# Last expert's bias products in its first layer and each normalisation one tile later; first expert's sums from its own rows

## The chip, the cores and the metric

The kernel runs on one NeuronCore of a Trainium2 chip. The metric is the device time of one execution in microseconds, the median of several. Its engines work side by side and meet at semaphores: TensorE (PE, with its weight loads as PEld), VectorE (DVE), ScalarE (ACT), GpSimd (POOL) and SyncE (SP). POOL issues the indirect DMAs (rows picked by an index), SP the plain loads. "POOLq" and "SPq" are the sequencers of these engines.

## The reference

One transformer layer on 4 x 1024 tokens of width 256: attention with 16 heads, an add and a layer norm, then a mixture of 8 experts, top 2, capacity 1280 rows each, an add and a layer norm. The change touches the second half only:

```python
x = _layernorm(x + attention(x))                       # (4, 1024, 256)
gates = softmax(x_flat @ router_w + router_b)          # (4096, 8)
expert_mask = one_hot(top2(gates)).sum(1)
pos = cumsum(expert_mask, axis=0) - 1                  # a token's slot in its expert
valid = expert_mask * (pos < capacity) > 0
buf[e, pos] = x_flat[token]                            # 8 x 1280 rows
h = gelu(buf[e] @ w1[e] + b1[e])
out = h @ w2[e] + b2[e]
y[token] = sum over its experts e of gates[token, e] * out[e, pos]
x = _layernorm(x + y)
```

## The kernel before, in words

`attention` (lines 144 to 1448) computes the first half. It leaves, in HBM, every token's row in `dispatched` (a row of 265 numbers for each slot of each expert: the token's 256 values, its 8 gates, its number) and in `sum_scratch`, where one row per token starts as the token's own values and collects the experts' outputs. Slots that no token fills hold zeros and an index of their own, behind the tokens.

`experts` (lines 1465 to 1903) handles the eight experts one after another, each 1280 rows as ST = 5 tiles of 128. LAST is expert 7. fp32 products are made of three (high by high, high by low, low by high), so every operand is split into a high part (ScalarE) and a remainder (VectorE). Per expert e:

- SP (`load_rows`, `load_weights`) loads the expert's rows into `rows[e % 2]` and its two weight matrices into `raw1`, `raw2`, in program order on one queue: rows of e, first weights of e, second weights of e, rows of e + 1. From expert 2 on, rows wait for `s_index >= e - 1` (line 1523).
- TensorE runs the first layer, 8 blocks m of 12 matmuls into `hp` (line 1663), then the second, 5 tiles t, each 8 high products (line 1629) and 8 low ones (line 1639) into `yp`. Between the tiles it transposes the next expert's rows (line 1617). Tile t waits until VectorE has read `yp` of tile t - 2 (`s_z`, line 1625).
- ScalarE applies Gelu to each block (line 1742) and copies the high part (line 1748), then takes the logarithm and exponential for the inverse deviations of the expert before (`rstd_guess`, lines 1717 and 1719), splits the next expert's weights and rows, and normalises the outputs of the expert before (`normalise`, line 1727).
- VectorE makes each block's remainder (line 1878), the index of the rows after block 1 (`index`), and, behind blocks 2 to 6, the statistics of the expert before (`variance`, lines 1824 and 1825; `tell_variances`, line 1829). In the second layer, for each tile: `prepare` (line 1845) puts gate times output bias onto the sums gathered from `sum_scratch`, into `others`; `add_own` (lines 1854 and 1856) adds gate times `yp`, into `eo`. `scale_and_shift` does one Newton step on the inverse deviation (lines 1459 to 1462) and the shift (line 1836).
- POOL, in its own fixed order: gathers the five tiles of sums (`gather_sums`, line 1557), tile t behind block t + 3 of the first layer; stores the new sums (`store_sums`, line 1565) and the normalised rows of the expert before (`store_outputs`, line 1574). A store of sums by one expert is waited for before the next expert gathers.

So the normalised rows of every expert are stored to `out`; the last expert that holds a token writes its final row. The last expert has no successor to hide behind: there VectorE works tile by tile (lines 1889 to 1902): `prepare` t, then (from tile 1) the Newton step of tile t - 1, for which it waits on ScalarE, `add_own` t, statistics of t. ScalarE answers each tile with `rstd_guess` and `normalise` (lines 1765 to 1767), and POOL stores it. `link` makes VectorE wait for the end of one of its own instructions before the next.

```python
                    if e == LAST and t:
                        scale_and_shift(LAST + t - 1, e, slice(t - 1, t))
```

The functions that the change touches:

Of the kernel before, what the change touches and what calls it, by code (L numbers as in the profile page):

```python
# [9 lines left out]
ALU = mybir.AluOpType  # L10
# [4 lines left out]
BATCH, SEQ, DIM, HEADS = 4, 1024, 256, 16  # L15
# [1449 lines left out]
def experts(nc, w1_d, b1_d, w2_d, b2_d, tile_d, disp_d, sum_d, ident, areas, out):  # L1465

    with ExitStack() as ctx:
# [40 lines left out]
        s_gather = [sem(f"s_gather{t}") for t in range(ST)]  # L1508
        s_sum, s_out = sem("s_sum"), sem("s_out")
        s_var, s_rstd, s_shift, s_final = sem("s_var2"), sem("s_rstd2"), sem("s_shift"), sem("s_final")  # L1510
        s_chain, s_actchain = sem("s_chain2"), sem("s_actchain2")
        block = ctx.enter_context(nc.Block())

# [4 lines left out]
        @block.sync  # L1518
        def _(sp):
            def load_rows(e):  # L1520
                if e >= 2:

                    sp.wait_ge(s_index, e - 1)
                sp.dma_start(rows[e % 2], disp_d[e * CAP:(e + 1) * CAP].rearrange("(t p) d -> p t d", p=P)
                             ).then_inc(s_rows[e % 2], 16)

            def load_weights(e):
                if e >= 2:

                    sp.wait_ge(s_w1lo, KC * (e - 1))  # L1530
                else:
                    sp.wait_ge(s_first_lo, KC)
                sp.dma_start(raw1, w1_d[e].rearrange("(k p) n -> p k n", p=P)).then_inc(s_w1, 16)
                if e >= 2:

                    sp.wait_ge(s_w2lo, KC * (e - 1))
                else:
                    sp.wait_ge(s_first_lo, 2 * KC)
                sp.dma_start(raw2, w2_d[e].rearrange("(k p) n -> p k n", p=P)).then_inc(s_w2, 16)

            for t in range(ST):
                sp.dma_start(rows[0][:, t], disp_d[P * t:P * (t + 1)]).then_inc(s_first[t], 16)
            sp.dma_start(b1[:], b1_d).then_inc(s_b1, 16)
            sp.dma_start(tile_no[:], tile_d).then_inc(s_tile, 16)
            load_rows(1)
            load_weights(1)
            sp.dma_start(b2[:].rearrange("p e d -> p (e d)"), b2_d.to_broadcast((P, EXPERTS * DIM))
                         ).then_inc(s_bias, 16)
            for e in range(2, EXPERTS):
                load_rows(e)  # L1550
                load_weights(e)

        @block.gpsimd
        def _(pool):
            def gather_sums(e, t):

                pool.indirect_dma_start(  # L1557
                    others[:, t, :], None, sum_d,
                    bass.IndirectOffsetOnAxis(ap=add_idx[e % 3][:, t:t + 1], axis=0),
                    bounds_check=TOKENS + CAP - 1).then_inc(s_gather[t], 16)  # L1560

            def store_sums(e, t):

                pool.wait_ge(s_z, ST * e + t + 1)
                pool.indirect_dma_start(  # L1565
                    sum_d, bass.IndirectOffsetOnAxis(ap=add_idx[e % 3][:, t:t + 1], axis=0),
                    eo[e % 2][:, t, :], None, bounds_check=TOKENS + CAP - 1).then_inc(s_sum, 16)

            def store_outputs(e, t):

                pool.wait_ge(s_final, ST * e + t + 1)
                if t == 0 and e:
                    pool.wait_ge(s_out, 16 * ST * e)
                pool.indirect_dma_start(  # L1574
                    rows_out, bass.IndirectOffsetOnAxis(ap=add_idx[e % 3][:, t:t + 1], axis=0),
                    eo[e % 2][:, t, :], None, bounds_check=TOKENS - 1, oob_is_err=False).then_inc(s_out, 16)

            for e in range(EXPERTS):
                if e:
                    store_sums(e - 1, ST - 1)  # L1580
                if e >= 2:
                    pool.wait_ge(s_h, HK * e + 2)
                    store_outputs(e - 2, 3)
                pool.wait_ge(s_index, e + 1)
                if e:
                    pool.wait_ge(s_sum, 16 * ST * e)
                    pool.wait_ge(s_z, ST * e)
                for t in range(ST):
                    pool.wait_ge(s_h, HK * e + 3 + t)
                    gather_sums(e, t)  # L1590
                if e >= 2:
                    pool.wait_ge(s_h, HK * (e + 1))
                    store_outputs(e - 2, 4)
                for t in range(ST - 1):
                    if e < LAST:
                        store_sums(e, t)
                    if e and t:
                        store_outputs(e - 1, t - 1)
            for t in range(ST - 2, ST):
                store_outputs(LAST - 1, t)  # L1600
            for t in range(ST):
                store_outputs(LAST, t)
            pool.wait_ge(s_out, 16 * ST * EXPERTS)
# [85 lines left out]
        def _(act):  # L1689
# [74 lines left out]
                    act.preload_act_table(ACT.Gelu)  # L1764
            for t in range(ST):
                rstd_guess(LAST + t, LAST, slice(t, t + 1))
                normalise(LAST + t, LAST, (t,))

        @block.vector
        def _(dve):  # L1770
            links = [0]

            def link(ins):
                links[0] += 1
                ins.then_inc(s_chain, 1)
                dve.wait_ge(s_chain, links[0])
# [50 lines left out]
            def tell_variances(n, e, T):  # L1827

                dve.tensor_scalar(lnt[e % 2][:, 0, T], mv[e % 2][:, T, 1], EPS, None, ALU.add).then_inc(s_var, 1)
                dve.wait_ge(s_var, n + 1)  # L1830

            def scale_and_shift(n, e, T):

                dve.wait_ge(s_rstd, n + 1)
                newton(dve, link, lnt[e % 2][:, :, T])
                dve.scalar_tensor_tensor(lnt[e % 2][:, 5, T], mv[e % 2][:, T, 0], -1.0, lnt[e % 2][:, 4, T],
                                         ALU.mult, ALU.mult).then_inc(s_shift, 1)

            def prepare(e, t):

                n, g = ST * e + t, gate[e % 2][:, t:t + 1]
                if n == 0:
                    dve.wait_ge(s_bias, 16)
                dve.wait_ge(s_gather[t], 16 * (e + 1))
                link(dve.scalar_tensor_tensor(others[:, t, :], b2[:, e, :], g, others[:, t, :], ALU.mult, ALU.add))  # L1845

            def add_own(e, t):

# [22 lines left out]
            for e in range(EXPERTS):  # L1871
                for m in range(HK):
# [8 lines left out]
                        index(e)  # L1881
                    if e and 2 <= m < 2 + ST:
                        variance(e - 1, m - 2)
                if e:
                    tell_variances(e - 1, e - 1, slice(0, ST))
                for t in range(ST):
                    if e + 1 < EXPERTS and t >= 2:
                        turned(e + 1, t)
                    prepare(e, t)
                    if e and t == 0:  # L1890
                        scale_and_shift(e - 1, e - 1, slice(0, ST))
                    if e == LAST and t:
                        scale_and_shift(LAST + t - 1, e, slice(t - 1, t))
                    add_own(e, t)
                    if e + 1 < EXPERTS:
                        if t < 2:
# [3 lines left out]
                    if e == LAST:  # L1900
                        variance(e, t)
                        tell_variances(LAST + t, e, slice(t, t + 1))
            scale_and_shift(LAST + ST - 1, LAST, slice(ST - 1, ST))


# [54 lines left out]
```

## Time and profile before

| | |
|---|---|
| time, median of 3 runs | 938.64 us (938.22 to 940.34) |
| time of the profiled execution | 938.71 us |
| its span, first to last instruction | 936.93 us |
| the experts' part of the span | 681.3 to 936.9 us |
| PE busy / DVE busy / ACT busy / POOL busy | 95% / 68% / 78% / 53% |
| granted TensorE clock, mean | 0.981 |

The span starts at the first instruction, and times below count from there in microseconds. The time of an execution is the span and some 1.8 us around it. A timeline row shows start, duration, engine, line, operation, the tile written and the tiles read, and in square brackets how long the engine had been idle and what ended that. Lines of the changed kernel are higher by 1 to 22: L1829 there is L1834, L1845 is L1867, L1854 is L1876, L1856 is L1878, L1717 is L1721, L1727 is L1731, L1574 is L1578.

### The profile page before, as it was taken

To read this page: it belongs to the slowest core of one execution; us is meant where nothing else is said; L and a number is where in the kernel's file an instruction comes from. 1 tells how busy PE (TensorE), PEld (TensorE's weight loads), DVE (VectorE), ACT (ScalarE), POOL (GpSimd) and SP (SyncE) were. 2 spreads that over 40 slices of the span, in tenths; PEclk is the share of its full clock that TensorE was granted. 3 is DMA by queue.
4 is the path that set the end of the run, shared out by engine and by line. 5 is a ranking of instruction groups with operands and counts; after the bars stand their busy time and mean duration, and the time that the engine had idled before them with its cause. 6 is when DMAs were issued, how large, how long until landed. Compare 5 with 4: busy or idle time off the path is not lost. (4 is left out here: it accounts for less than half of the span.)

```text
span 936.9 us, 19456 instructions
## 1 busy us (share of the span) xinstructions
PE 893.0 (95%) x7345; PEld 508.7 (54%) x7345; DVE 635.9 (68%) x1193; ACT 731.7 (78%) x894; POOL 496.1 (53%) x412
## 2 busy tenths in 40 slices
PE   8899998999999999999999999999589999999994
PEld 5434343434334434333443433344489999998993
DVE  5678555557886655889565676437457877888876
ACT  6688977897797899789789879987265787777863
POOL 5478344245475745747564444522623656656564
PEclk9899999999999999999999999999799999999998
DMA  5724495442446335253433426531274435534311
GB/s 175 171 89 159 144 302 192 146 166 96 154 141 226 114 132 215 84 197 124 163 129 133 146 97 207 167 105 36 90 242 138 134 131 176 175 137 140 121 60 56
DMA packets 62713, 136.08 MB, mean 145 GB/s; under 512 B 10370, under 2 KB 31427, under 8 KB 62480
## 3 DMA queue, kind: packets, MB, share of 16 engines
q1 hardware_dynamic: 41936, 72.88, 23.9%
q0 software_dynamic: 20672, 61.83, 19.1%
q8 instruction: 61, 1.00, 0.4%
q14 instruction: 44, 0.36, 0.1%
HBM read 69.85 MB, written 62.35 MB: 141 GB/s over the span
## 5 line engine op out<-in xcount | busy, mean ns | idle before, releaser
L788 ACT ACTIVATE prob<-spsum 128x1024 f32<-128x1024 f32 x512 | 493.6, 1022 | 92.0 <-PE spsum L992 86.2
L1016 PE MATMUL opsum<-prob,val 128*17 128x512 f32 x2048 | 271.3, 599 | 3.0 <-DVE oraw L1391 2.2
L992 PEld LDWEIGHTS spsum<-stacks 32*128 32x128 f32 x1536 | 73.7, 184 | 116.3 <-ACT prob L788 63.6
L992 PE MATMUL spsum<-stacks 32*128 32x512 f32 x1536 | 133.3, 427 | 3.0 <-DMA stacks<-split_scratch 2.4
L992 PEld LDWEIGHTS spsum<-area_q 32*128 32x128 f32 x1536 | 73.6, 185 | 112.3 <-ACT prob L788 65.3
L992 PE MATMUL spsum<-area_q 32*128 32x512 f32 x1536 | 133.3, 429 | 0.8 <-ACT prob L788 0.7
L1399 DVE RECIPROCAL oden<-oden 128x256 f32<-128x256 f32 x62 | 108.7, 1753 | 2.1
L667 POOL TENSOR_TENSOR onorm<-oraw,oden 128x512 f32<-128x512 f32 x31 | 42.0, 1356 | 104.9 <-DVE oden L1399 104.8
L581 POOL TENSOR_TENSOR area_s<-emb,area_s 128x1024 fp32r<-128x1024 f32 x28 | 66.6, 2380 | 50.2 <-DVE area_s L1210 50.2
L625 POOL DMA_INDIRECT dispatched<-res,scatter_idx x64 | 64.9, 1014 | 48.1 <-issue 24.7
L579 POOL TENSOR_TENSOR square<-raw 128x512 bf16<-128x512 f32 x28 | 53.9, 1924 | 58.5 <-DVE raw L1190 58.4
L1016 PEld LDWEIGHTS opsum<-prob,val 128*17 128x17 f32 x2048 | 36.1, 95 | 89.2 <-ACT prob L788 51.5
L1557 POOL DMA_INDIRECT others<-sum_scratch,add_idx x40 | 57.0, 1424 | 42.2 <-PE hp L1663 41.3
L1742 ACT ACTIVATE hraw<-hp,b 128x640 f32<-128x640 f32 x64 | 51.0, 797 | 31.8 <-PE hp L1663 30.6
L1878 DVE TENSOR_TENSOR hid<-hraw,hid 128x640 fp32r<-128x640 f32 x64 | 52.8, 825 | 29.9 <-ACT hid L1748 29.9
L1565 POOL DMA_INDIRECT sum_scratch<-eo,add_idx x35 | 44.1, 1261 | 44.5 <-DVE eo L1856 36.9
L1391 DVE COPY oraw<-opsum 128x512 f32<-128x512 f32 x31 | 21.4, 692 | 58.1 <-PE opsum L1016 57.7
L1663 PE MATMUL hp<-xe,area_s 128*128 128x320 f32 x384 | 57.1, 309 | 0.5 <-DVE xe L1788 0.5
L1663 PE MATMUL hp<-xe,w1s 128*128 128x320 f32 x384 | 57.0, 308 | 0.0
L1663 PEld LDWEIGHTS hp<-xe,area_s 128*128 128x128 f32 x384 | 56.4, 188 | 0.7 <-issue 0.7
L1663 PEld LDWEIGHTS hp<-xe,w1s 128*128 128x128 f32 x384 | 56.4, 188 | 0.0
L1574 POOL DMA_INDIRECT out<-eo,add_idx x40 | 41.7, 1042 | 25.6 <-issue 13.7
(246 smaller groups left out, 1371.0 us busy)
## 6 DMA issues: line engine op xcount, KB each, us to landing
split_scratch<-area_s POOLq DMA_DIRECT2D x56, 512.0 KB, 4.1
area_k<-in_w SPq DMA_DIRECT2D x16, 1024.0 KB, 5.3
area_q<-split_scratch SPq DMA_DIRECT2D x28, 512.0 KB, 5.6
stacks<-split_scratch SPq DMA_DIRECT2D x24, 512.0 KB, 5.3
dispatched<-res POOLq DMA_DIRECT2D x1, 5300.0 KB, 27.8
rows<-dispatched SPq DMA_DIRECT2D x7, 662.5 KB, 5.4
res<-in_x SPq DMA_DIRECT2D x4, 1024.0 KB, 8.6
aT<-onorm SPq DMA_DIRECT2D x124, 32.0 KB
```

The costliest lines, as they stand in the source:

```text
L579: pool.tensor_tensor(square[:, i], raw[:], raw[:], ALU.mult).then_inc(s_square, 1)
L581: pool.tensor_tensor(split[u % 2][:, 1], embs[u % 2][:], split[u % 2][:, 0].bitcast(F32), ALU.subtract).then_inc(s_split, 1)
L625: pool.indirect_dma_start(disp_d, bass.IndirectOffsetOnAxis(ap=scatter_idx[:, k, t:t + 1], axis=0), ress[UNITS[u][0] % 2][:, t, :], None, ...
L788: act.activation(prob[u % NPB][:], spsum[u % NSB][:].rearrange("p a n -> p (a n)"), ACT.Exp, scale=HD ** -0.5).then_inc(s_exp, 1)
L992: ins = pe.matmul(spsum[u % NSB][:, j % 2, :], kst[par][rows, a, P * kt:P * (kt + 1)], qst[par][rows, b, cols], start=i == 0, stop=i == 2 ...
L1016: ins = pe.matmul(opsum[32 * j:32 * j + HD + 1, :], val[b % 2][:, kt, h0 + j, :], prob[(2 * s + j // 2) % NPB][:, HALF * (j % 2):HALF * (j ...
L1399: tell(dve.reciprocal(half, half), s_sums)
L1557: pool.indirect_dma_start(others[:, t, :], None, sum_d, bass.IndirectOffsetOnAxis(ap=add_idx[e % 3][:, t:t + 1], axis=0), bounds_check=TOK ...
L1565: pool.indirect_dma_start(sum_d, bass.IndirectOffsetOnAxis(ap=add_idx[e % 3][:, t:t + 1], axis=0), eo[e % 2][:, t, :], None, bounds_check= ...
L1663: ins = pe.matmul(hp[n % 2][:, h, 0:CH], w1s[e % 2][:, b, k, P * m:P * (m + 1)], xe[e % 2][:, a, k, CH * h:CH * (h + 1)], start=k == 0 and ...
L1742: act.activation(hraw[n % NH][:].rearrange("p (h n) -> p h n", h=2), hp[n % 2][:, :, 0:CH], ACT.Gelu, bias=b1[:, e, m:m + 1]).then_inc(s_g ...
L1878: dve.tensor_tensor(hids[:, 1, m], hraw[n % NH][:], hids[:, 0, m].bitcast(F32), ALU.subtract).then_inc(s_hid, 1)
```

## The change

Three things, all in `experts`:

1. *Last expert, bias products.* `prepare` of tiles 0, 1 and 2 moves into the first layer, behind blocks 5, 6 and 7; that of tiles 3 and 4 runs behind the statistics of tiles 0 and 1.
2. *Last expert, scales.* The Newton step and shift of tile t - 1 (`finish_tile`, new, with the first two of its instructions merged into one) run behind the statistics of tile t, not ahead of `add_own` of t. On ScalarE the normalisation of tile t - 1 follows `rstd_guess` of tile t. Tile 4 is normalised by VectorE itself, in one `tensor_scalar` on the tile, and its store waits for the new semaphore `s_tail`.
3. *First expert.* No gathers: `prepare` reads the expert's own rows in `rows[0]` (no expert has added anything yet). Those rows are now read until the end of expert 0, so expert 2's rows, which go to the same place, wait for `s_index >= 2` instead of 1; and `s_gather` counts one expert less.

```diff
--- before.py
+++ after.py
@@ -1508,6 +1508,7 @@
         s_gather = [sem(f"s_gather{t}") for t in range(ST)]
         s_sum, s_out = sem("s_sum"), sem("s_out")
         s_var, s_rstd, s_shift, s_final = sem("s_var2"), sem("s_rstd2"), sem("s_shift"), sem("s_final")
+        s_tail = sem("s_tail")
         s_chain, s_actchain = sem("s_chain2"), sem("s_actchain2")
         block = ctx.enter_context(nc.Block())
 
@@ -1520,7 +1521,7 @@
             def load_rows(e):
                 if e >= 2:
 
-                    sp.wait_ge(s_index, e - 1)
+                    sp.wait_ge(s_index, max(e - 1, 2))
                 sp.dma_start(rows[e % 2], disp_d[e * CAP:(e + 1) * CAP].rearrange("(t p) d -> p t d", p=P)
                              ).then_inc(s_rows[e % 2], 16)
 
@@ -1568,7 +1569,10 @@
 
             def store_outputs(e, t):
 
-                pool.wait_ge(s_final, ST * e + t + 1)
+                if e == LAST and t == ST - 1:
+                    pool.wait_ge(s_tail, 1)
+                else:
+                    pool.wait_ge(s_final, ST * e + t + 1)
                 if t == 0 and e:
                     pool.wait_ge(s_out, 16 * ST * e)
                 pool.indirect_dma_start(
@@ -1585,7 +1589,7 @@
                 if e:
                     pool.wait_ge(s_sum, 16 * ST * e)
                     pool.wait_ge(s_z, ST * e)
-                for t in range(ST):
+                for t in range(ST if e else 0):
                     pool.wait_ge(s_h, HK * e + 3 + t)
                     gather_sums(e, t)
                 if e >= 2:
@@ -1764,7 +1768,8 @@
                     act.preload_act_table(ACT.Gelu)
             for t in range(ST):
                 rstd_guess(LAST + t, LAST, slice(t, t + 1))
-                normalise(LAST + t, LAST, (t,))
+                if t:
+                    normalise(LAST + t - 1, LAST, (t - 1,))
 
         @block.vector
         def _(dve):
@@ -1829,6 +1834,21 @@
                 dve.tensor_scalar(lnt[e % 2][:, 0, T], mv[e % 2][:, T, 1], EPS, None, ALU.add).then_inc(s_var, 1)
                 dve.wait_ge(s_var, n + 1)
 
+            def finish_tile(e, t):
+
+                n, T = LAST + t, slice(t, t + 1)
+                v, guess, w, rstd, shift = (lnt[e % 2][:, i, T] for i in (0, 2, 3, 4, 5))
+                dve.wait_ge(s_rstd, n + 1)
+                link(dve.scalar_tensor_tensor(w, guess, guess, v, ALU.mult, ALU.mult))
+                link(dve.tensor_scalar(w, w, -0.5, 1.5, ALU.mult, ALU.add))
+                link(dve.tensor_tensor(rstd, guess, w, ALU.mult))
+                if t < ST - 1:
+                    dve.scalar_tensor_tensor(shift, mv[e % 2][:, t, 0:1], -1.0, rstd, ALU.mult, ALU.mult
+                                             ).then_inc(s_shift, 1)
+                else:
+                    dve.tensor_scalar(eo[e % 2][:, t, :], eo[e % 2][:, t, :], mv[e % 2][:, t, 0:1], rstd,
+                                      ALU.subtract, ALU.mult).then_inc(s_tail, 1)
+
             def scale_and_shift(n, e, T):
 
                 dve.wait_ge(s_rstd, n + 1)
@@ -1841,8 +1861,10 @@
                 n, g = ST * e + t, gate[e % 2][:, t:t + 1]
                 if n == 0:
                     dve.wait_ge(s_bias, 16)
-                dve.wait_ge(s_gather[t], 16 * (e + 1))
-                link(dve.scalar_tensor_tensor(others[:, t, :], b2[:, e, :], g, others[:, t, :], ALU.mult, ALU.add))
+                if e:
+                    dve.wait_ge(s_gather[t], 16 * e)
+                sums = others[:, t, :] if e else rows[0][:, t, 0:DIM]
+                link(dve.scalar_tensor_tensor(others[:, t, :], b2[:, e, :], g, sums, ALU.mult, ALU.add))
 
             def add_own(e, t):
 
@@ -1881,16 +1903,17 @@
                         index(e)
                     if e and 2 <= m < 2 + ST:
                         variance(e - 1, m - 2)
+                    if e == LAST and m >= HK - 3:
+                        prepare(e, m - (HK - 3))
                 if e:
                     tell_variances(e - 1, e - 1, slice(0, ST))
                 for t in range(ST):
                     if e + 1 < EXPERTS and t >= 2:
                         turned(e + 1, t)
-                    prepare(e, t)
+                    if e < LAST:
+                        prepare(e, t)
                     if e and t == 0:
                         scale_and_shift(e - 1, e - 1, slice(0, ST))
-                    if e == LAST and t:
-                        scale_and_shift(LAST + t - 1, e, slice(t - 1, t))
                     add_own(e, t)
                     if e + 1 < EXPERTS:
                         if t < 2:
@@ -1900,7 +1923,11 @@
                     if e == LAST:
                         variance(e, t)
                         tell_variances(LAST + t, e, slice(t, t + 1))
-            scale_and_shift(LAST + ST - 1, LAST, slice(ST - 1, ST))
+                        if t + 3 < ST:
+                            prepare(e, t + 3)
+                        if t:
+                            finish_tile(e, t - 1)
+            finish_tile(LAST, ST - 1)
 
 
 def kernel(L0_attn_x, L0_attn_wq, L0_attn_wk, L0_attn_wv, L0_attn_wo, L0_attn_pope_bias,
```

VectorE, first layer of the last expert from the statistics behind block 5 to the first own product of the second layer. L1878 is a block's remainder, L1824 and L1825 the statistics of expert 6, L1829 their telling, L1845 the bias product, L1459 to L1836 the Newton step of expert 6. Before:

```order
L1824 BN_STATS stats<-eo 128x6
L1825 BN_AGGR mv_0<-stats 128x2
L1878 TENSOR_TENSOR hid<-hraw,hid 128x640
L1824 BN_STATS stats<-eo 128x6
L1825 BN_AGGR mv_0<-stats 128x2
L1878 TENSOR_TENSOR hid<-hraw,hid 128x640
L1829 TENSOR_SCALAR lnt_0<-mv_0 128x5
L1845 SCALAR_TENSOR_TENSOR others<-b,gate,others 128x256
L1459 TENSOR_TENSOR lnt_0<-lnt_0 128x5
```

In the changed kernel, where L1900 is the remainder, L1829 and L1830 are the statistics, L1867 is the bias product and L1834 the telling:

```order
L1829 BN_STATS stats<-eo 128x6
L1830 BN_AGGR mv_0<-stats 128x2
L1867 SCALAR_TENSOR_TENSOR others<-b,gate,others 128x256
L1900 TENSOR_TENSOR hid<-hraw,hid 128x640
L1829 BN_STATS stats<-eo 128x6
L1830 BN_AGGR mv_0<-stats 128x2
L1867 SCALAR_TENSOR_TENSOR others<-b,gate,others 128x256
L1900 TENSOR_TENSOR hid<-hraw,hid 128x640
L1867 SCALAR_TENSOR_TENSOR others<-b,gate,others 128x256
L1834 TENSOR_SCALAR lnt_0<-mv_0 128x5
L1459 TENSOR_TENSOR lnt_0<-lnt_0 128x5
```

Three bias products stand ahead of the telling now; the one that stood between it and the Newton step is gone.

VectorE, second layer of the last expert, one tile in the middle. Before:

```order
L1845 SCALAR_TENSOR_TENSOR others<-b,gate,others 128x256
L1459 TENSOR_TENSOR lnt_1<-lnt_1 128x1
L1460 TENSOR_TENSOR lnt_1<-lnt_1 128x1
L1461 TENSOR_SCALAR lnt_1<-lnt_1 128x1
L1462 TENSOR_TENSOR lnt_1<-lnt_1 128x1
L1836 SCALAR_TENSOR_TENSOR lnt_1<-mv_1,lnt_1 128x1
L1854 SCALAR_TENSOR_TENSOR others<-yp,gate,others 128x256
L1856 SCALAR_TENSOR_TENSOR eo<-yp,gate,others 128x256
L1824 BN_STATS stats<-eo 128x6
L1825 BN_AGGR mv_1<-stats 128x2
L1829 TENSOR_SCALAR lnt_1<-mv_1 128x1
```

In the changed kernel, the last tile and the end (L1842 to L1846 are `finish_tile` of tile 3, the second L1842 begins that of tile 4, L1849 is its scale):

```order
L1876 SCALAR_TENSOR_TENSOR others<-yp,gate,others 128x256
L1878 SCALAR_TENSOR_TENSOR eo<-yp,gate,others 128x256
L1829 BN_STATS stats<-eo 128x6
L1830 BN_AGGR mv_1<-stats 128x2
L1834 TENSOR_SCALAR lnt_1<-mv_1 128x1
L1842 SCALAR_TENSOR_TENSOR lnt_1<-lnt_1 128x1
L1843 TENSOR_SCALAR lnt_1<-lnt_1 128x1
L1844 TENSOR_TENSOR lnt_1<-lnt_1 128x1
L1846 SCALAR_TENSOR_TENSOR lnt_1<-mv_1,lnt_1 128x1
L1842 SCALAR_TENSOR_TENSOR lnt_1<-lnt_1 128x1
L1843 TENSOR_SCALAR lnt_1<-lnt_1 128x1
L1844 TENSOR_TENSOR lnt_1<-lnt_1 128x1
```

The five small instructions stood between the telling of a tile and the next own product and belonged to the tile just told; now they are four, and up to tile 3 they belong to the tile before it.

## Rows read from the trace of the kernel before

**Rows 1.** Page, busy time and share of the span, TensorE.

```profile
PE 893.0 (95%) x7345; PEld 508.7 (54%) x7345; DVE 635.9 (68%) x1193; ACT 731.7 (78%) x894; POOL 496.1 (53%) x412
```

**Rows 2.** Chain that ended last, its end: start us, us, what.

```profile
927.58 0.61 ACT eo L1727
928.24 3.12 issue
...
932.64 0.98 POOL out L1574
```

**Rows 3.** Timeline, VectorE, last expert's second layer, from tile 3's L1854 to tile 4's.

```profile
924.17 0.48 DVE L1854 SCALAR_TENSOR_TENSOR others<-yp,gate,others 128x256 f32<-128x256 f32 x1
...
925.88 0.15 DVE L1829 TENSOR_SCALAR lnt<-mv 128x1 f32<-128x1 f32 x1
...
926.61 0.16 DVE L1459 TENSOR_TENSOR lnt<-lnt 128x1 f32<-128x1 f32 x1
...
927.46 0.48 DVE L1854 SCALAR_TENSOR_TENSOR others<-yp,gate,others 128x256 f32<-128x256 f32 x1
```

**Rows 4.** Timeline, TensorE, tile 2 of the last expert's second layer.

```profile
914.67 2.14 PE L1629 MATMUL yp<-w2s,hid 128*128 128x512 f32 x8
...
916.64 1.10 PE L1639 MATMUL yp<-w2s,hid 128*128 128x256 f32 x8
```

**Rows 5.** Timeline, VectorE and ScalarE, end of the last expert's first layer.

```profile
909.03 0.82 DVE L1878 TENSOR_TENSOR hid<-hraw,hid 128x640 fp32r<-128x640 f32 x1 [0.38 <-ACT hid L1748]
...
910.79 0.83 DVE L1878 TENSOR_TENSOR hid<-hraw,hid 128x640 fp32r<-128x640 f32 x1 [0.38 <-ACT hid L1748]
...
911.54 0.17 DVE L1829 TENSOR_SCALAR lnt<-mv 128x5 f32<-128x5 f32 x1
...
912.00 0.21 ACT L1717 ACTIVATE lnt<-lnt 128x5 f32<-128x5 f32 x1
...
913.61 0.48 DVE L1854 SCALAR_TENSOR_TENSOR others<-yp,gate,others 128x256 f32<-128x256 f32 x1
```

**Rows 6.** DMA, 720 to 745 us: GB/s in 40 slices, totals, issues to landing.

```profile
GB/s 0 72 138 98 238 383 374 382 341 248 354 401 142 101 141 20 151 59 0 164 46 0 203 7 0 0 0 0 0 0 66 144 0 0 0 223 0 203 13 111
DMA packets 2147, 3.01 MB, mean 121 GB/s; under 512 B 176, under 2 KB 1840, under 8 KB 2144
...
rows<-dispatched SPq DMA_DIRECT2D x1, 662.5 KB, 5.6
others<-sum_scratch,add_idx POOLq DMA_INDIRECT x5, 3.3
```

**Rows 7.** Source view of L1330: ns min/median/max, first and last start, shape.

```profile
L1330 DVE TENSOR_SCALAR res<-res,mv,lnt x28: 411/416/2583, 256.3 to 645.5; 128x256 f32<-128x256 f32 x28
```

**Rows 8.** Timeline, two executions of L1330 and POOL beside them.

```profile
273.46 3.03 DVE L1330 TENSOR_SCALAR res<-res,mv,lnt 128x256 f32<-128x256 f32 x2
...
273.50 2.38 POOL L581 TENSOR_TENSOR area_s<-emb,area_s 128x1024 fp32r<-128x1024 f32 x1 [1.86 <-DVE area_s L1210]
```

**Rows 9.** Timeline, VectorE and POOL: a store behind its tile; the last expert's stores.

```profile
718.00 0.48 DVE L1856 SCALAR_TENSOR_TENSOR eo<-yp,gate,others 128x256 f32<-128x256 f32 x1
...
719.27 1.33 POOL L1565 DMA_INDIRECT sum_scratch<-eo,add_idx  x1 [1.74 <-DVE eo L1856]
...
923.41 0.98 POOL L1574 DMA_INDIRECT out<-eo,add_idx  x1 [2.28 <-DMA out<-eo,add_idx]
...
931.36 0.98 POOL L1574 DMA_INDIRECT out<-eo,add_idx  x1 [4.40 <-issue]
```

**Rows 10.** Timeline, VectorE, first bias product of the first expert.

```profile
704.56 0.48 DVE L1845 SCALAR_TENSOR_TENSOR others<-b,gate,others 128x256 f32<-128x256 f32 x1
```

**Rows 11.** Timeline, SP, TensorE and ScalarE in the second expert.

```profile
723.86 0.37 SPq L1524 DMA_DIRECT2D rows<-dispatched  x1
...
731.30 0.38 PE L1617 MATMUL tp<-ident,rows 128*128 128x128 f32 x2
...
734.72 1.90 ACT L1695 CAST area_s<-area_k 128x2048 fp32r<-128x2048 f32 x1
```

## Prediction

> **What bounds the kernel now.** I read the page first, then the chain of waits, then the timeline of the last 30 us, POOL's stores in it, and last the load queue. TensorE is busy for 893.0 us of the 936.9 us span [rows 1], so the diff's edits, which leave every matmul alone, can pay only where TensorE doesn't set the pace. That is the end. The chain of waits leaves TensorE when the last expert's first layer ends at about 909.1; its last pieces are tile 3's normalisation on ScalarE, 3.12 us in which POOL stands ready and does nothing visible, and the store of tile 4 at 932.64 [rows 2]. From that store's start to the end of the span are 936.93 - 932.64 = 4.29 us.
>
> The pace before it is VectorE's. One tile, counted from L1854 to the next L1854, takes 927.46 - 924.17 = 3.29 us [rows 3]. In it: 1.71 us from L1854 to L1829 (add the own product, statistics, tell the variance); 0.73 us from L1829 to L1459, which is ScalarE's Ln and Exp and the way there and back, with L1845 (the bias product) inside it for free; 0.85 us from L1459 to the next L1854, the Newton step and the shift, five instructions. TensorE needs 914.67 to 916.64 + 1.10 = 917.74, so 3.07 us, for a tile of the second layer, and then waits [rows 4].
>
> **The change, term by term.** I call the start of tile t's L1854 D(t).
>
> *Last expert, first layer.* Three bias products (0.51 us each, 0.48 busy and the hand-over) move from the second layer into blocks 5, 6 and 7 of the first. Ahead of the next remainder VectorE is idle for 0.38 us [rows 5]. So products 0 and 1 push the remainders back by about 0.14 each, 0.29 together (each link costs a little too), and product 2 pushes L1829 by 0.51 more: 911.54 becomes 912.34. ScalarE notices: its Ln stood ready at 912.00, just behind the table load, and now starts when L1829 ends, 912.51. The Newton chain of expert 6 follows, and the bias product that used to lie in its wait is gone from there, so nothing is given back. D(0) goes from 913.61 to 914.14, **0.53 us later**. The gathers are issued one block after another, tile t's with block t + 3; its product now comes about three blocks of 1.76 us (the spacing of the two remainders) later, 5.3 us against 3.3 us to landing [rows 5, 6]. No wait there.
>
> *Second layer.* Between L1829 and the next L1854 now lie L1829 itself with the way to the next instruction, 0.19 (0.15 busy), then a bias product (0.51) behind tiles 0 and 1 only, then, from tile 1 on, the Newton step of the tile before. Its rstd was asked for a whole tile ago, so the 0.73 us of waiting is gone. Four instructions take 0.85 - 0.19 = 0.66. So
> D(1) = 914.14 + 1.71 + 0.19 + 0.51 = 916.55,
> D(2) = 916.55 + 1.71 + 0.19 + 0.51 + 0.66 = 919.62,
> D(3) = 919.62 + 2.56 = 922.18, D(4) = 924.74,
> where D(4) was 927.46 [rows 3]. TensorE stays ahead: with tile 2 starting at 914.67 + 0.53 [rows 4] and each tile some 2.9 us behind the last, its results come at about 918.3, 921.2 and 924.1, and the narrowest margin is 0.7 us at tile 4.
>
> *The end.* Tile 4's L1829 starts at 924.74 + 1.71 = 926.45. Tile 3's Newton step runs from 926.64 to 927.30; ScalarE's normalisation of tile 3 starts 0.12 later (927.46 to 927.58 before) [rows 2, 3] and ends at 928.02. Tile 4's Newton step and its scale, now on VectorE itself, take 0.58 + 0.41: the nearest row is L1330, the same operation on the same shape, 416 ns in the middle of its 28 [rows 7]. Tile 4 is ready at 928.29.
>
> *POOL.* A store starts 0.79 us after its tile is ready (718.48 to 719.27), and a store behind a store starts 0.30 after the other's 0.98 (932.64 against 931.36 + 0.98) [rows 2, 9]. Expert 6's outputs are 0.53 later, so the last expert's first store, which waits for them to land, goes from 923.41 to 923.94 [rows 9], and three more could follow by 927.8. Tile 3's store starts at 928.02 + 0.79 = 928.81 and ends at 929.79; tile 4's goes at 930.09, since it is ready long before. The span ends at 930.09 + 4.29 = 934.38, **2.5 us earlier** (932.64 - 930.09 = 2.55). The profiled execution took 938.71 us, 0.07 above the median of 938.64, so the sum gives 938.71 - 2.55 = 936.2 us. A tile may be off by a tenth; five tiles make that 0.5 us each way.
>
> *First expert.* Five gathers and their 0.66 MB go, and L1845 reads the rows instead. At 704.56 L1845 follows the remainder before it without a wait [rows 10], so the gathers held nobody: 0. The cover is the rest of the first layer; with it gone they would have cost their 3.3 us to landing [rows 6]. A new wait comes with it: the rows of expert 2 overwrite those of expert 0, so SP holds that load until the second index, which so far releases expert 3's rows at 723.86 [rows 11]. Behind it on the same queue wait both weight loads of expert 2 and the rows of expert 3. All four go then: 3.45 MB. Rows issued at 723.86 landed 5.6 us later with weights ahead of them, so expert 2's land by 729.5, against 731.30 where TensorE transposes them; at the 370 GB/s that the queue reaches in this stretch the first weights, 1.05 MB, follow in 2.8 us, at 732.3, against 734.72 where ScalarE splits them [rows 6, 11]. Covered by 1.8 and 2.4 us: 0. From expert 3 on the queue runs as before.
>
> **What speaks against the change.** The scale of the last tile is a one-input instruction of VectorE that reads and writes SBUF, while POOL writes descriptors. L1330 shows what company can do: 411 ns at best and 2583 ns at worst, and two of them took 3.03 us together while POOL subtracted two tiles beside them for 2.38 [rows 7, 8]. The Trainium skill ("SBUF — State Buffer", Who interferes with whom) states that such an instruction in a two-port mode and GpSimd exclude each other for a whole instruction, whoever comes second waiting. By that rule the last scale would wait out a store's descriptors if the two met, which by the working of the second rival makes 937.1 us instead of 936.2; the long rows of L1330 agree with it. By my times they don't meet: the scale runs from 927.88 to 928.29, 0.5 us ahead of tile 3's store.
>
> **Rivals.**
> *The 3.12 us return.* Tile 3 was ready at 928.18 and its store started at 931.36 [rows 2, 9], where 0.79 is usual. Nothing in the trace says why, and no other store or gather of the experts shows it. If it belongs to this place in the program, tile 3's store goes at 928.02 + 3.15 = 931.2, tile 4's at 932.5, and the kernel takes 938.6 us, the same as before. For it: an unexplained wait in exactly the place where the gain must pass. Against it: 1 of 40 output stores, and POOL does five DMAs fewer before it, so a cause that goes by count moves away.
> *The last scale meets a store.* It then ends after tile 3's descriptors, 929.79 + 0.41 = 930.20, tile 4's store starts at 930.99 instead of 930.09, and the time is 937.1.
> *The held loads arrive late.* This is the way to a slower kernel. ScalarE's split of expert 2's weights stands ahead of its transposed tiles, on which TensorE waits, so each microsecond past 734.72 is lost. If the burst moved no faster than the 121 GB/s that this stretch means over all its time [rows 6], with expert 1's gathers (0.66 MB) among it, rows, weights and gathers (2.38 MB) would take 19.7 us, the weights land at 743.6, 8.8 us late, and the kernel takes 936.2 + 8.8 = 945.0. It decides from 2.5 us of lateness, measurably from 4.4. Against it: the queue reached 370 to 400 GB/s whenever it had work here.
>
> **How the numbers follow.** A measurement of this kernel can tell about 0.2%, 1.9 us, from no change: faster is below 936.8, slower above 940.5. The forecast (936.2, by itself 935.6 to 936.9) gets 0.62, of which 0.06 falls above 936.8. The returning wait gets 0.24, all of it the same. The meeting at the port gets 0.08, half on each side of 936.8. The late loads get 0.06, nearly all slower. Sum: faster 0.59, same 0.35, slower 0.06. The range runs from the forecast's low end, 935.6, to the returning wait with its spread, 938.9.
>
> **What would show it.** Right: in the profile after, a VectorE period of about 3.1 us and then 2.56 us from L1876 to L1876 of the last tiles, with no wait for ScalarE before L1842 except perhaps the last; D(0) near 914.1; the two last stores near 928.9 and 930.1; the last TENSOR_SCALAR at 0.41 us; loads of expert 2's rows and weights together at about 723.9 and no wait of ScalarE for them. Wrong: the last two stores as late as 931 and 932, a gap of 3 us before tile 3's, VectorE waiting for TensorE's yp in tile 3 or 4, or ScalarE idle before the split at 734.7.

## The result, and the profile after

The changed kernel is slower, by 0.7%. The median is 946.63 us (945.71 to 947.83, 6 runs) against 938.56 us (938.22 to 940.34, 6 runs), ratio 1.0071, 95% interval 1.0052 to 1.0089. (The ratio is not the quotient of the two medians, which is 1.0086.) The forecast was 936.2 us, in a range from 935.6 to 938.9.

The profiled execution took 947.28 us, its span is 945.5 us. Busy shares hardly moved: the page's first part, to be read beside [rows 1].

```profile
PE 894.6 (95%) x7345; PEld 508.4 (54%) x7345; DVE 635.4 (67%) x1188; ACT 730.7 (77%) x893; POOL 489.9 (52%) x407
```

The second layer of the last expert runs as the working said. VectorE's timeline from tile 0's first own product to the last scale (columns as in [rows 3]):

```profile
917.42 0.48 DVE L1876 SCALAR_TENSOR_TENSOR others<-yp,gate,others 128x256 f32<-128x256 f32 x1
...
919.84 0.48 DVE L1876 SCALAR_TENSOR_TENSOR others<-yp,gate,others 128x256 f32<-128x256 f32 x1
...
922.98 0.47 DVE L1876 SCALAR_TENSOR_TENSOR others<-yp,gate,others 128x256 f32<-128x256 f32 x1
...
925.59 0.48 DVE L1876 SCALAR_TENSOR_TENSOR others<-yp,gate,others 128x256 f32<-128x256 f32 x1
...
928.20 0.48 DVE L1876 SCALAR_TENSOR_TENSOR others<-yp,gate,others 128x256 f32<-128x256 f32 x1
...
931.44 0.41 DVE L1849 TENSOR_SCALAR eo<-eo,mv,lnt 128x256 f32<-128x256 f32 x1
```

The periods are 2.42, 3.14, 2.61 and 2.61 us, where [rows 3] have 3.29. The pause of 3.12 us in front of tile 3's store [rows 2, 9] is gone too. POOL's timeline, its last three stores:

```profile
930.22 0.98 POOL L1578 DMA_INDIRECT out<-eo,add_idx  x1 [0.30 <-issue]
932.32 0.98 POOL L1578 DMA_INDIRECT out<-eo,add_idx  x1 [1.12 <-DVE eo L1849]
933.61 0.98 POOL L1578 DMA_INDIRECT out<-eo,add_idx  x1 [0.30 <-issue]
```

But the span goes on for 945.50 - 933.61 = 11.89 us behind the start of the last store; before it was 4.29. No engine is busy behind that store's own 0.98 us, and the chain of waits ends with the store as it did in [rows 2], so neither view shows the loss. The source view of line 1467 does, the line under which the instructions that close the second block are recorded (columns: engine, operation, count, then ns min/median/max, first and last start in us). The kernel before:

```profile
L1467 POOLq COMPARE_BRANCH  x1: 33/33/33, 935.1 to 935.1; - x1
L1467 POOLq DRAIN  x1: 1464/1464/1464, 935.2 to 935.2; - x1
```

The changed kernel:

```profile
L1467 PEldq DRAIN  x1: 3125/3125/3125, 924.1 to 924.1; - x1
L1467 ACTq DRAIN  x1: 632/632/632, 930.9 to 930.9; - x1
L1467 DVEq DRAIN  x1: 448/448/448, 931.5 to 931.5; - x1
L1467 POOLq COMPARE_BRANCH  x1: 33/33/33, 936.1 to 936.1; - x1
L1467 POOLq DRAIN  x1: 9059/9059/9059, 936.2 to 936.2; - x1
```

**GpSimd's closing DRAIN takes 9.06 us instead of 1.46**. It starts right behind the branch at 936.1, which waits until the last stores have landed. The other engines' DRAINs end before it starts.

The two spans differ by 8.57 us. TensorE's DRAIN that closes the attention starts at 680.88 before and 683.14 after (+2.26); from there to the last expert's first matmul of `hp` are 213.97 and 215.11 us (+1.14); from that matmul (894.85 and 898.25) to the last store's start 37.79 and 35.36 (-2.43); behind it 4.29 and 11.89 (+7.60). The last two terms are the change's. The first lies where the programs are the same; in the other profiled runs that DRAIN starts anywhere between 676.2 and 681.9, whatever the edit. The second wanders too, between 213.3 and 216.1 us over all runs, so that +1.14 can't be put down to the change either. What is free of both is the stretch from the last expert's first `hp` matmul to the end of the span: 936.93 - 894.85 = 42.08 us before, 945.50 - 898.25 = 47.25 after. The table below has it for every run.

### The profile page after: what moved, and what is told of

Same layout as the page of the kernel before. It is cut to its first block and busy times, and to the rows that moved or that the text cites. A ratio compares the mean times of both kernels' runs of the same rounds, so it can differ in the third digit from the quotient of the medians.

```text
span 945.5 us, 19438 instructions
## 1 busy us (share of the span) xinstructions
PE 894.6 (95%) x7345; PEld 508.4 (54%) x7345; DVE 635.4 (67%) x1188; ACT 730.7 (77%) x893; POOL 489.9 (52%) x407
## 5 line engine op out<-in xcount | busy, mean ns | idle before, releaser
L1900 DVE TENSOR_TENSOR hid<-hraw,hid 128x640 fp32r<-128x640 f32 x64 | 52.8, 825 | 29.9 <-ACT hid L1752 29.8
L1558 POOL DMA_INDIRECT others<-sum_scratch,add_idx x35 | 50.9, 1453 | 24.1 <-PE hp L1667 23.8
```

The lines of the kernel that those rows point to most:

```text
L1558: pool.indirect_dma_start(others[:, t, :], None, sum_d, bass.IndirectOffsetOnAxis(ap=add_idx[e % 3][:, t:t + 1], axis=0), bounds_check=TOK ...
L1900: dve.tensor_tensor(hids[:, 1, m], hraw[n % NH][:], hids[:, 0, m].bitcast(F32), ALU.subtract).then_inc(s_hid, 1)
```

## The experiments

Each ran beside the kernel before on one and the same chip, and its ratio is to the runs beside it. The table at the end has the rows in one place; POOL's gathers and stores (DMA_INDIRECT) are numbered from 0 in it, attention's included, so that tile 3's last store before is number 177 of 179.

**Each part alone.** `a_first` is the kernel before with the first expert's part (no gathers, sums from the rows, the held load); `b_last` is everything else.

> The kernel before with the first expert's part alone: no gathers in expert 0, expert 2's rows held until the second index. Theory 1 (the long end belongs to the five DMAs that POOL no longer issues): POOL's DRAIN takes about 9 us as in the changed kernel, and the time is about 938.6 + 7.6 = 946 us. Theory 2 (it belongs to the last expert's new order or to its last store's new semaphore): DRAIN stays at 1.5 us and the time at 938.6 us within 1 us.

> The kernel before with the last expert's part alone, the five gathers of expert 0 and the old wait of the load kept. Theory 1 (count of POOL's DMAs): DRAIN 1.5 us, and the gain of the last expert's part shows whole: 938.6 - 2.6 = 936.0 us. Theory 2 (last expert's order or semaphore): DRAIN about 9 us, time about 936 + 7.6 = 943.6 us or more.

Measured: `a_first` 1.0104 [1.0079, 1.0128], DRAIN 9.06 us, no pause at the store; `b_last` 1.0014 [0.9994, 1.0034], DRAIN 1.46 us, and the pause still there:

```profile
923.86 0.98 POOL L1578 DMA_INDIRECT out<-eo,add_idx  x1 [0.30 <-issue]
928.49 0.98 POOL L1578 DMA_INDIRECT out<-eo,add_idx  x1 [3.65 <-issue]
929.77 0.98 POOL L1578 DMA_INDIRECT out<-eo,add_idx  x1 [0.30 <-issue]
```

So the first expert's part makes the DRAIN long and takes the pause away; the last expert's part does neither, and its gain is swallowed by the pause: from the first `hp` matmul to the end are 42.07 us in `b_last`, where the kernel before has 42.08.

**Restoring the number of DMAs with unused gathers.** The changed kernel plus 5 (`spare5`) or 2 (`spare2`) gathers in expert 0:

```diff
+ for t in range(5 if e == 0 else 0):
+     pool.wait_ge(s_h, HK * e + 3 + t)
+     (gather of sums into eo[1][:, t], then_inc(s_spare, 16))
+ if e == 0: pool.wait_ge(s_spare, 16 * 5)
```

(VectorE waits for them too, in expert 1, before it writes to `eo[1]`.)

> The changed kernel with five gathers put back into expert 0, at the same places, into a buffer that nobody reads (their data is not used; the results are still computed from the rows). Theory 1 (count): DRAIN 1.5 us, about 936 us. Rival 3 (the held load of expert 2 or the rows as the source of the sums, not the missing DMAs, cause the long end): DRAIN stays at 9 us, about 946.6 us. Theory 2 also says 946.6.

> The same with two unused gathers instead of five, a point between. Theory 1 in its plain form (each DMA of POOL shifts a piece of housekeeping by one place): DRAIN somewhere between 1.5 and 9 us, or the pause of some 3 us before one of the last stores, as in the kernel before. Theories 2 and 3: DRAIN 9 us, 946.6 us.

Measured: `spare5` 1.0076 [1.0051, 1.01] with a DRAIN of 9.06 us, `spare2` 1.0052 [1.0029, 1.0074] with 9.22 us. The number alone doesn't decide.

**Place in the stream, or the DMAs.** `after_keep` keeps expert 0's own five gathers unused (`for t in range(ST)`, and VectorE waits for `s_gather[t]`). `after_w30` and `after_w15` add to the changed kernel, `last_w2` adds to `b_last`:

```diff
+ for _ in range(30 if e == 0 else 0):      # 15 in after_w15, 2 in last_w2
+     pool.wait_ge(s_h, 3)
```

> The changed kernel with expert 0's five gathers put back on GpSimd and left unused (the bias products still read the rows themselves; VectorE only waits for the gathers). GpSimd's instruction stream is then that of the kernel before, word for word; the held row load and the sums from the rows stay. Theory 4 (what GpSimd issues, by its place in its own stream, decides how long its last DRAIN takes): DRAIN 1.46 us instead of 9.06, the pause of 3.15 us before tile 3's last store is back, and the time is that of the version with the last expert's part alone, 0.998 to 1.003 of before. Rival 3 (the held load of the rows, or VectorE reading them, is the cause): DRAIN 9.06 us, ratio 1.007.

> The version with the last expert's part alone (DRAIN 1.46 us, pause 3.15 us), plus two waits on GpSimd in expert 0 that are satisfied already: one more instruction in its stream, no more DMAs, no data changed. Theory 4 in its strict form (the place counted in instructions decides): DRAIN 9.06 us, the 3.15 us pause gone, ratio 1.006 to 1.009, as in the run with five spare gathers, whose stream was longer by one instruction too. Theory 5 (it is what GpSimd's DMAs leave in the descriptor queue, counted in DMAs and their kinds, and the spare gathers differed in that): DRAIN 1.46 us, ratio about 1.000.

> The changed kernel plus thirty waits on GpSimd in expert 0 that are satisfied already, in the place of the five gathers: fifteen instructions, as many as the gathers had, so that every later instruction of GpSimd stands at the place it had before the change; no DMA added. Theory 4 (place in the stream): DRAIN 1.46 us, the 3.15 us pause back, time at most that of before, ratio 0.996 to 1.003. Theory 5 (DMAs): DRAIN 9.06 us as in the changed kernel, ratio 1.007.

> The changed kernel plus fifteen such waits, seven instructions: the length of the stream of the run with two spare gathers. Theory 4: the same pauses as there (about 1.6 us at the store of expert 0's sums, 1.1 and 1.6 us later) and DRAIN about 9.2 us, though no DMA is added. Theory 5: pauses and DRAIN of the changed kernel, 1.6 us once and 9.06 us.

Measured: `after_keep` 1.0003 [0.9989, 1.0017], DRAIN 1.46 us; `last_w2` 1.0003 [0.999, 1.0015], 1.46 us; `after_w30` 1.0054 [1.0034, 1.0074], 9.06 us; `after_w15` 1.0075 [1.0046, 1.0105], 9.06 us. Rival 3 falls by the first: with the held load and the rows as sums both in place the DRAIN is short. The place in the stream falls by the other three: moving every later instruction by 1, 7 or 15 places changes neither number. The Trainium skill ("Runtime: NRT & Kernel Launch", Instruction fetch mechanics) says that the cost of passing an instruction block's end is mostly hidden; in these three runs no cost of a place shows, the DRAIN and the pause being what they were (9.06, and 1.46 with 3.15).

**Is it the DRAIN at all?** The second block without it, and one more DRAIN ahead of the last expert's five stores:

```diff
-        block = ctx.enter_context(nc.Block())
+        block = ctx.enter_context(nc.Block(no_gpsimd_drain=True))   # after_nodrain, before_nodrain
```
```diff
+            pool.drain()                                            # after_early
             for t in range(ST):
                 store_outputs(LAST, t)
```

> The changed kernel with its second block opened without GpSimd's closing DRAIN (all stores are still waited for by their semaphore before). Theory 6 (the loss is that DRAIN, 9.06 us against 1.46 in the kernel before, and nothing behind it needs the time): from the last store's start to the end 11.89 - 9.06 = 2.8 us, and the time about 937.5 - 1.46 - 2.5 = 0.995 to 0.998 of before. Rival (the DRAIN only shows a wait that the end of the program has in any case): the span ends 11.9 us behind the last store as now, ratio 1.005 to 1.008.

> The kernel before with its second block opened without GpSimd's closing DRAIN. Theory 6: its 1.46 us go, ratio 0.9985 (0.997 to 1.000), the pause of 3.15 us at tile 3's store stays. Rival: no difference, and the wait shows somewhere else.

> The changed kernel with one more DRAIN on GpSimd, ahead of the last expert's five stores. If the 9.06 us are work that piles up and is done once (or code that is met for the first time), the early DRAIN takes about 9 us and the last one 1.5 us or less; the early one then lies beside the last expert's second layer in part, and holds the stores of tiles 0 and 1. If they are what a DRAIN takes in this kernel, both take about 9 us. Ratio 1.000 to 1.003 by the first, 1.007 and over by the second.

> The changed kernel with expert 0's gathers kept (DRAIN 1.46 us, pause 3.15 us), and GpSimd waiting for their arrival before it goes on, as it does in the run with five spare gathers, which had the long DRAIN with the same number of DMAs. Theory 5a (GpSimd's clearing of finished transfers goes by when it waits for them): DRAIN 9.06 us, the 3.15 us pause gone. Theory 5b (kinds and targets of the DMAs decide): DRAIN 1.46 us, pause 3.15 us.

Measured: `after_nodrain` 932.14 us against 937.01, ratio 0.9956 [0.9937, 0.9976]; its span ends 930.49 - 927.69 = 2.80 us behind the last store. `before_nodrain` 0.9991 [0.9974, 1.0009], with the same 2.80 us. `after_early` 1.0045 [1.0027, 1.0064]; its two DRAINs (source view):

```profile
L1605 POOLq DRAIN  x1: 12821/12821/12821, 912.9 to 912.9; - x1
```
```profile
L1467 POOLq DRAIN  x1: 467/467/467, 934.4 to 934.4; - x1
```

The length is paid once: the early DRAIN took 12.82 us and left 0.47 for the last. It starts at 912.91 beside DMAs that POOL is still working on, the last of which ends at 917.07, so 8.66 of the 12.82 us lie behind them. It held up the stores behind it:

```profile
916.09 0.98 POOL L1578 DMA_INDIRECT out<-eo,add_idx  x1 [0.30 <-issue]
926.61 0.98 POOL L1578 DMA_INDIRECT out<-eo,add_idx  x1 [9.53 <-issue]
```

From the first `hp` matmul to the end are 44.86 us: 2.4 less than in the changed kernel, but still 2.8 more than before. The ratio lies above the 1.000 to 1.003 that was expected. `keep_wait`, which makes POOL wait for expert 0's gathers, has 1.46 us and the pause, 1.0013 [0.9995, 1.0031]: when POOL waits is not what decides.

**How many, and which.** What decides the length was still open, so six more ran: `keep4` and `keep2` keep four and two of the gathers, `twice` makes all five a second time into the same tiles, `spare5_nowait` is `spare5` without POOL's wait, `keep_eo` has the kept gathers write where the spare ones did, `last_nodrain` is `b_last` without the DRAIN.

> The changed kernel with four of expert 0's five gathers kept (178 of GpSimd's gathers and stores, where the kernel before has 179 and the changed one 174). If one DMA less is enough to move the pause off tile 3's store and the cost into the DRAIN: DRAIN about 9 us, no 3.15 us pause, ratio 1.005 to 1.008. If the cost moves with a threshold further down: DRAIN 1.46 us, the pause at tile 4's store or at the same instruction, ratio about 1.000.

> The changed kernel with two of expert 0's five gathers kept (176 DMAs, as in the run with two spare gathers, which had a DRAIN of 9.22 us). By a count of DMAs alone: the pauses of that run (DMA 66, 99, 145, counted from 0) and DRAIN 9.22 us. If the targets matter too: another pattern; DRAIN about 9 us in either case, unless the threshold lies below 176.

> The changed kernel with expert 0's five gathers kept and then made a second time, into the same tiles: 184 of GpSimd's gathers and stores, ten more than in the changed kernel. In the five runs with a DRAIN of 1.46 us of which the expectation is based, and in the one with 178 DMAs, the long pause met the DMA with number 177, counted from 0 (before: the last but one; with 178 DMAs: the last). Theory 7 (a fixed number of these DMAs is where the cost falls, and if the kernel ends short of it the DRAIN pays 9 us): the pause now meets number 177, a store of the last expert but one or of tile 0 that nobody waits for, DRAIN 1.46 us, and neither is on the way to the end: last store 9.5 us behind PE's end instead of 11.9, ratio 0.996 to 1.000. If the pause stays at tile 3's store, the count is wrong; if the DRAIN takes 9 us, so is the idea that it is paid once.

> As the run with five spare gathers into the other expert's output tiles (179 DMAs, DRAIN 9.06 us), but GpSimd does not wait for them; VectorE alone does. What GpSimd issues now differs from the kernel with expert 0's gathers kept (DRAIN 1.46 us) only in where five gathers write and in the semaphore they count. If GpSimd's own extra instruction turned it: DRAIN 1.46 us and a 3.15 us pause. If the targets or the semaphore did: DRAIN 9.06 us.

> Expert 0's five gathers kept with their own semaphores, but written into the other expert's output tiles, as the spare gathers were (those had semaphores of their own, and a DRAIN of 9.06 us with 179 DMAs). If where they write decides: DRAIN 9.06 us, pause about 1 us at DMA 177. If the semaphore did: DRAIN 1.46 us, pause 3.15 us.

> The last expert's part alone (gathers of expert 0 as before), second block without GpSimd's closing DRAIN. The pause of 3.15 us at tile 3's store stays, so most of that part's gain stays hidden: span behind the last store 2.80 us, ratio 0.998 (0.996 to 1.000), some 2.5 us above the changed kernel without the DRAIN (0.9956). If it comes to 0.9956 too, the first expert's part gives nothing once the DRAIN is gone.

With 178 DMAs the pause meets number 177 again, now tile 4's store, and the DRAIN is short. POOL's timeline in `keep4`:

```profile
932.34 0.98 POOL L1578 DMA_INDIRECT out<-eo,add_idx  x1 [1.08 <-DVE eo L1849]
935.26 0.98 POOL L1578 DMA_INDIRECT out<-eo,add_idx  x1 [1.94 <-issue]
```

With 184 it falls among stores that nobody waits for, number 177 has 0.29 us more than its neighbours, and the last two go straight through. The DRAIN is short all the same, and the forecast's gain shows: from the first `hp` matmul to the end are 39.63 us, 2.45 less than before. `twice`:

```profile
921.86 0.98 POOL L1578 DMA_INDIRECT out<-eo,add_idx  x1 [0.59 <-issue]
...
931.05 0.98 POOL L1578 DMA_INDIRECT out<-eo,add_idx  x1 [0.45 <-issue]
932.33 0.98 POOL L1578 DMA_INDIRECT out<-eo,add_idx  x1 [0.30 <-issue]
```

| kernel | POOL's DMAs | idle at no. 177 | DRAIN | first `hp` to end | ratio to before |
|---|---|---|---|---|---|
| before | 179 | 3.15 | 1.46 | 42.08 | 1 |
| b_last, after_keep, keep_wait, last_w2 | 179 | 3.15 | 1.46 | 42.06 to 42.12 | 1.0003 to 1.0014 |
| keep_eo | 179 | 3.15 | 1.46 | 42.05 | one run |
| keep4 | 178 | 1.94 | 1.46 | 41.32 | 1.0015 [0.9999, 1.0031] |
| twice | 184 | 0.59 | 1.46 | 39.63 | 0.997 [0.9955, 0.9985] |
| keep2, spare2 | 176 | - | 9.22 | 47.44, 47.44 | one run; 1.0052 |
| after, after_w30, after_w15 | 174 | - | 9.06 | 47.25 to 47.33 | 1.0054 to 1.0075 |
| a_first | 174 | - | 9.06 | 49.15 | 1.0104 [1.0079, 1.0128] |
| spare5, spare5_nowait | 179 | 0.98 | 9.06 | 47.50, 47.51 | 1.0076; one run |
| after_early | 174 | - | 12.82, 0.47 | 44.86 | 1.0045 [1.0027, 1.0064] |
| before_nodrain | 179 | 3.15 | none | 40.59 | 0.9991 [0.9974, 1.0009] |
| last_nodrain | 179 | 3.15 | none | 40.59 | 0.9993 [0.9976, 1.001] |
| after_nodrain | 174 | - | none | 38.19 | 0.9956 [0.9937, 0.9976] |

(Times in us. The idle time is counted from when POOL could start: from its own release, behind which 0.76 is usual, or from the preceding DMA's end, behind which 0.30 is. Above the usual are 2.39 of the 3.15, 1.64 of the 1.94, 0.29 of the 0.59 and 0.22 of the 0.98.) With the closing DRAIN in place, every kernel of this family that reaches number 177 has the short DRAIN and every one that ends short of it the long one, with one exception: spare gathers that count a semaphore of their own. `spare5_nowait` differs from `keep_eo` on POOL only by that semaphore (one for all five gathers, where `keep_eo` has the tiles' own five), and has 9.06 us against 1.46; VectorE's wait for the gathers moved as well, and each is a single run. To leave the spare gathers out of the count doesn't mend it: `spare2` has the 9.22 us of `keep2`, which has two real gathers more than the changed kernel, and not its 9.06. Why the semaphore should matter no run tells. Nor does one tell what GpSimd does in the 9 us: the records show a duration and no reason. That the pause at number 177 and the 7.6 us are the same work, done early or late, is a guess that the sizes speak against: in `twice` number 177 has 0.29 us above the usual and the DRAIN is 7.6 us shorter, in `spare5` it has nearly the same 0.22 and the DRAIN is long.

## Why the prediction was wrong

**The step that failed** is the last term of the sum, "The span ends at 930.09 + 4.29 = 934.38": the 4.29 us from the last store's start to the end of the span were carried over from the kernel before, unchanged and without a reason. They are 11.89 us in the changed kernel, and all of the difference is in one instruction that the chain of waits doesn't list, GpSimd's closing DRAIN (9.06 us instead of 1.46). With it fails the 0 that the working gives to the first expert's part: its five gathers held nobody, as said, but leaving them out costs 7.6 us at the other end of the program (`after_keep` puts only them back, and the DRAIN is short). Without the DRAIN the changed kernel comes to 0.9956, with it to 1.0071; the kernel before comes to 0.9991 without it.

**VectorE's pace: right.** Forecast periods 2.41, 3.07, 2.56, 2.56; measured 2.42, 3.14, 2.61, 2.61. D(0) was to be 0.53 later; from the first `hp` matmul it is 19.17 us instead of 18.76, so 0.41.

**The end before the DRAIN: right.** From that matmul to the last store 2.43 us less, forecast 2.55; to the end of the span 38.19 us in `after_nodrain` against 40.59 in `before_nodrain`, 2.40 less. The last scale took 0.41 us, 931.44 to 931.85, and tile 3's store started at 932.32, so the second rival's meeting did not take place.

**The returning wait: half right.** The rival put the 3.12 us to a place in the program, and against it that "a cause that goes by count moves away". The count it was: the pause stays in `b_last`, goes with the gathers, and meets number 177 again in `keep4`. Without the DRAINs, last part alone 0.9993, both parts 0.9956: it is the first expert's part that lets the last expert's gain through. What the working didn't ask is what else would change with the count.

**The held loads: right.** Timeline of SP and ScalarE after the change:

```profile
726.71 0.37 SPq L1525 DMA_DIRECT2D rows<-dispatched  x1
727.12 0.53 SPq L1534 DMA_DIRECT2D area_k<-in_w  x1
```
```profile
737.46 0.21 ACT L1723 ACTIVATE lnt<-lnt 128x5 f32<-128x5 f32 x1
737.57 1.89 ACT L1699 CAST area_s<-area_k 128x2048 fp32r<-128x2048 f32 x1
```

The split of the weights follows ScalarE's exponential without a wait.

**The median moved by more than this.** 8.07 us between the medians, against 7.60 - 2.43 = 5.2 from the change's own places. The ratio's interval is 4.9 to 8.4 us of 938.56, so 5.2 is inside it. In the profiled runs the rest, 3.4 us, lies ahead of the last expert, where runs of every kernel here differ by as much. A part of it may go with the clock granted to TensorE: 0.979 on average against 0.981 before. Of the runs of the kernel before beside `keep4`, one had a span of 938.2 us at a granted clock of 0.979 and one of 932.9 us at 0.986; by estimate from these two, 0.002 less is 1.5 us. No run was aimed at the rest, and it stays open.

## What to carry to other kernels

Compare the whole stretch from the last useful instruction to the span's end, closing instructions included; a chain of waits that ends at the last transfer says nothing of it. Where an unexplained pause goes by a count of DMAs, taking DMAs away in front of it can change something else as well: here five fewer made the closing DRAIN 7.6 us longer, and five more than before, of no use otherwise, gave 0.997. Where the last stores are waited for by their semaphores anyway, opening the block without GpSimd's DRAIN is worth a try first: it turned this change from 1.0071 into 0.9956, the lowest ratio of those that ran. It pays where the DRAIN is long; with the 1.46 us of the kernel before it gave 0.9991 [0.9974, 1.0009], no measurable gain.

## What the runs showed of the hardware

GpSimd's DRAIN at the end of this block has a few fixed lengths: 1.464 us in eight kernels, 9.059 in six, 9.222 in two, the same to the nanosecond from kernel to kernel, and 12.821 and then 0.467 us in the one that has two. The Trainium skill ("VectorE: DVE Perf Modes", The DRAIN you can't avoid) gives about 12 ns, on all engines, for the DRAINs that the runtime puts at a program's start and end. Those of this kernel's closing block are recorded under a line of the kernel, so it isn't shown that they are of that kind, and they are longer: 0.12 us on SyncE, 0.19 to 0.52 on VectorE, 0.63 on ScalarE, 3.03 to 3.14 on TensorE and up to 9.22 on GpSimd. GpSimd's pause before indirect DMA number 177 is as regular: 3.15 us in eight kernels. Neither moved when instructions without a DMA were added.
